# A woven four-layer transformer kernel: one shared round order replaced by an order of its own per engine, with the back half first

## The chip, the cores and the metric

The kernel runs on one core of one Trainium2 chip. The metric is the device time of one launch in microseconds. Before the change it is 4669.69 us, the median of 3 runs (4665.78 to 4671.7). A difference is given against that median.

## What is computed

Input are 16 sequences of 256 tokens with 128 features, and the weights of eight residual steps, taken one after another:

```python
x = L0_attn_x
x = x + _L0_attn_ref(_layernorm(x), ...)   # causal softmax attention, 16 heads of 8
x = x + _L0_ffn_ref(_layernorm(x), ...)    # top-2 of 8 experts with a capacity, hidden 512
x = x + _L1_attn_ref(_layernorm(x), ...)   # causal softmax attention
x = x + _L1_ffn_ref(_layernorm(x), ...)    # shared-key attention (4 heads) and top-2 of 8 gated experts
x = x + _L2_attn_ref(_layernorm(x), ...)   # causal linear attention (relu)
x = x + _L2_ffn_ref(_layernorm(x), ...)    # causal softmax attention and a gated MLP
x = x + _L3_attn_ref(_layernorm(x), ...)   # attention with weights (1 + arccos(cos))**-3.2
x = x + _L3_ffn_ref(_layernorm(x), ...)    # three blocks: linear + LoRA, layernorm, gelu, linear + LoRA
```

All matrices are float32. A sequence needs nothing of another one.

## The kernel before

Two sequences (512 tokens) make a pass, and there are 8 passes. Features lie on the 128 partitions, tokens along the free side. The work of a pass is cut in two **halves**, each with buffers of its own and four of the eight PSUM banks (the class Half): the **front** half holds the first four residual steps (stages causal0, moe0, causal1, mqa and moe1, list FRONT, L182), the **back** half the last four (linear, causal2, mlp, arccos, qlora and block0 to block2, list BACK, L184). Front hands its sum to back at its end (L1432 writes back_x). `run` (L1524) writes, for each engine, front of pass 0 alone, then a loop of 7 turns that holds front of pass i+1 and back of pass i, then back of pass 7 alone. In a turn the two halves depend on each other only at the end of the turn, where front writes back_x for the next turn.

The halves meet on the same three engines. TensorE (PE) runs all matmuls, ScalarE (ACT) exponentials, copies and table functions, VectorE (DVE) maxima, masks and sums. Every engine executes its instructions in the order in which they were written, so the order in which the two halves' instructions are written decides who waits for whom. Each half is a set of generators, one for each stage and engine (`headed_pe`, `arccos_act` and so on), that yield a **round number** before each group of instructions. SHARES (L169) gives a weight to each kind of round, PHASES (L170) says how many rounds a stage has. `schedule` (L189) lays the rounds of both halves on one axis from 0 to 1 by these weights and sorts them; `weave` (L204) lets each half write all its instructions up to that round. The sorted list is the same for all three engines. So both halves advance in proportion and end together.

The stages that matter here: a causal stage first takes the row maxima of all scores (`max_pe` L583 on PE, reductions L627 on DVE), then 12 weights sets (`causal_scores_pe` L657: scores, an exponential on ACT at L767, then `causal_pv_pe` L685). moe0 has 16 rounds (`moe0_pe` L1326) of two matmuls into the hidden layer (L1338), two relus on ACT (L1359) and two matmuls out (L1346). arccos works on four **units** (half the heads of one sequence): `arccos_act` (L1099) runs six passes over a buffer of 4096 columns for each unit, a logarithm (L1134), tanh, square root and arctangent (L1132), a logarithm and an exponential, each of which needs the one before. Functions of different tables need a table load between them. When the six passes of a unit are done, DVE sums the buffer (`arccos_sums_dve` L1137) and PE multiplies with the values (`arccos_pv_pe` L1085, L1094). The two buffers alternate between the units.

At the start SyncE issues all loads (`load`, L1540) in the order masks, const, input of pass 0, causal0, lora, the integer weights, then the other stages, qlora last. PE first multiplies the LoRA factors (L1593), and DVE builds the effective weights weff from the integer weights, the scales and that product (L1624 to L1632). PE waits for weff and for the qlora load before it starts on front of pass 0, though only the back half reads them:

```python
            last.then_inc(lora_ps, 1)
            pe.wait_ge(weff_ready, 1)
            pe.wait_ge(loaded["qlora"], 16)
            run(pe, {...
```

Of the kernel before, what the change touches and what calls it, by code (L numbers as in the profile page):

```python
# [107 lines left out]
class Signal:  # L108
# [56 lines left out]
NORM_ROUNDS = 2  # L165
PROJECT = 3
ROUTE = 5
OUT = 3
SHARES = {"norm": 1, "project": 3.14, "maxima": 2.36, "weights": 0.98, "linear": 2, "out": 1.38, "queries": 1.5, "route": 1.8, "experts0": 1.8, "experts1": 1.2, "mlp": 1.2, "arc_in": 2.3, "arc": 2.3, "block": 1}  # L169
PHASES = {  # L170
    "norm": [(NORM_ROUNDS, "norm")],
    "causal": [(PROJECT, "project"), (MROUNDS + 1, "maxima"), (CSETS + 1, "weights"), (OUT, "out")],
    "linear": [(PROJECT, "project"), (ESETS + 1, "linear"), (OUT, "out")],
    "mqa": [(1, "project"), (TILES + 1, "maxima"), (QSETS, "queries"), (3, "out")],
    "moe0": [(ROUTE, "route"), (FSETS + 1, "experts0")],
    "moe1": [(ROUTE, "route"), (EXPERTS + 2, "experts1")],
    "mlp": [(5, "mlp")],
    "arccos": [(6, "arc_in"), (UNITS * ARC_STEPS + 2, "arc"), (OUT, "out")],
    "block": [(3 + NORM_ROUNDS, "block")],
}  # L180
ROUNDS = {kind: sum(n for n, _ in phases) for kind, phases in PHASES.items()}
# [7 lines left out]
def schedule(halves):  # L189


    order = []
    for h, parts in enumerate(halves):
        times = [SHARES[phase] for kind, _ in parts for n, phase in PHASES[kind] for _ in range(n)]
        at = 0.0
        for r, time in enumerate(times):
            order.append(((at + time / 2) / sum(times), h, r))
            at += time
        if parts is FRONT:
            order[-1] = (1.0, h, r)  # L200
    return [(h, r) for _, h, r in sorted(order)]
# [10 lines left out]
def in_rounds(parts, turn, stage_of):  # L212

    first = 0
    for kind, name in parts:
        for r in stage_of[kind](turn, name):
            yield first + r
        first += ROUNDS[kind]

# [164 lines left out]
def build(nc, x_dram, w_dram, qw_dram, out_dram):  # L384
    cols, width = columns()
    with ExitStack() as ctx:
# [50 lines left out]
        def norm_pe(pe, h, turn, n, first=0):  # L437
# [7 lines left out]
            if gain:  # L445
                pe.wait_ge(loaded[gain], 16)
# [1298 lines left out]
```

## Time and profile before

| | |
|---|---|
| median of 3 runs | 4669.69 us (4665.78 to 4671.7) |
| profiled execution, its own time | 4677.62 us |
| its span, first to last instruction | 4675.8 us |
| busy in the span: PE, ACT, DVE | 3620.7, 2342.1, 1741.4 us |
| front of pass 0 alone, first matmul to the loop | 34.87 to 403.70 us |
| 7 turns of the loop | 403.70 to 4294.37 us |
| back of pass 7 alone | 4294.37 us to the end |
| mean granted TensorE clock | 0.787 of full |

The table is read from the page of the profile and from the timeline of PE: the loop starts and ends where the first matmul of the back half (L442 on back_x) starts. DMA matters only in the first 35 us; after that 1 to 6 GB/s are moved.

### The profile page before, as it was taken

The page shows a single profiled execution, that of the slowest core. Times are in us where ns is not written, and L with a number is a line of the kernel's source. Part 1 is how long each engine was busy: PE and PEld are TensorE (multiplying, and loading weights), DVE is VectorE, ACT ScalarE, POOL GpSimd, SP SyncE. Part 2 cuts the span into 40 slices and gives each one's busy share as a digit, 9 for nine tenths or more (in the row PEclk, how much of TensorE's full clock was granted, in tenths as well). Part 3 has the DMA queues.
Part 4 walks back from the last instruction along what each step waited for, and adds up shares of the span by engine and source line. Part 5 has one row for each costly group of instructions (what it writes and reads, how often), then busy time and mean ns, then how long its engine had stood idle before and what let it go on. Part 6 is the DMA issues. An engine that isn't in the chain of part 4 may idle for free.

```text
span 4675.8 us, 48868 instructions
## 1 busy us (share of the span) xinstructions
PE 3620.7 (77%) x19372; PEld 1949.4 (42%) x19372; DVE 1741.4 (37%) x2541; ACT 2342.1 (50%) x2177; POOL 3.8 (0%) x11
## 2 busy tenths in 40 slices
PE   5878886788767987678977888678876798767834
PEld 2445443454334543335434444345433454333411
DVE  2225333343433434344243533334343343433332
ACT  2223348543684436743475435844368443674275
POOL 0000000000000000000000000000000000000000
PEclk8858896788867897588966989578886779858766
DMA  2000000000000000000000000000000000000000
GB/s 113 1 1 3 1 1 1 0 6 1 1 1 5 1 1 1 1 6 1 1 1 1 6 1 1 1 0 6 1 1 1 3 1 1 1 1 3 1 0 3
DMA packets 4578, 20.31 MB, mean 4 GB/s; under 512 B 608, under 2 KB 864, under 8 KB 3808
## 3 DMA queue, kind: packets, MB, share of 16 engines
q1 hardware_dynamic: 4320, 16.79, 0.9%
q8 instruction: 171, 2.80, 0.3%
q14 instruction: 87, 0.71, 0.1%
HBM read 14.70 MB, written 2.10 MB: 4 GB/s over the span
## 4 chain that ended last, share of the span: by engine, by line
PE 57%; ACT 22%; DVE 12%; issue 8%; DMA 1%; SPq 0%; DVEq 0%; ACTq 0%
ACT back_cosines L1132 6%; PE front_ps L1338 5%; PE front_ps L1346 5%; PE front_ps L1226 3%; PE back_ps L1094 3%; ACT back_cosines L1134 3%; PE front_ps L1388 3%; PE back_ps L724 2%; DVE back_nsum L1141 2%; ACT L1132 2%; PE back_ps L821 2%; PE front_ps L975 2%; ACT L1521 2%; PE front_ps L693 2%; PE back_ps L516 2%
## 5 line engine op out<-in xcount | busy, mean ns | idle before, releaser
L1132 ACT ACTIVATE back_cosines<-back_cosines 128x4096 f32<-128x4096 f32 x128 | 462.7, 3615 | 1.4
L767 ACT ACTIVATE front_scratch<-front_ps 128x1152 f32<-128x1152 f32 (+1 forms) x192 | 196.1, 1021 | 207.9 <-PE front_ps L679 207.7
L1359 ACT ACTIVATE front_scratch<-front_ps,wts 128x512 f32<-128x512 f32 x256 | 173.4, 686 | 192.4 <-PE front_ps L1338 190.4
L1134 ACT ACTIVATE back_cosines<-back_cosines,wts 128x4096 f32<-128x4096 f32 x64 | 236.9, 3701 | 63.0 <-DVE back_cosines L1189 62.8
L1338 PE MATMUL front_ps<-front_xn,wts 128*128 128x512 f32 x512 | 247.3, 606 | 9.3 <-DVE front_qk L1322 8.5
L627 DVE TENSOR_REDUCE front_negm<-front_ps 128x4 f32<-128x1024 f32 (+1 forms) x192 | 228.4, 1219 | 61.5 <-PE front_ps L601 60.3
L1346 PE MATMUL front_ps<-front_scratch,wts 128*128 128x512 f32 x512 | 240.5, 592 | 0.0
L668 PE MATMUL front_ps<-ident_bf,mask_q 128*128 128x256 bf16 x512 | 114.3, 338 | 129.8 <-ACT front_scratch L767 88.5
L532 ACT ACTIVATE back_cosines<-back_ps,wts 128x512 fp32r<-128x512 f32 (+1 forms) x136 | 120.6, 887 | 174.1 <-PE back_ps L516 41.9
L733 PE MATMUL back_ps<-zero_bf,ident_bf 128*128 128x512 bf16 x128 | 63.3, 495 | 176.7 <-DVE back_vs L1150 160.3
L532 ACT ACTIVATE front_scratch<-front_ps,wts 128x512 fp32r<-128x512 f32 (+1 forms) x152 | 128.6, 860 | 135.1 <-PE front_ps L608 60.7
L1141 DVE TENSOR_REDUCE back_nsum<-back_cosines 128x8 f32<-128x2048 f32 x64 | 143.2, 2281 | 114.0 <-ACT back_cosines L1132 114.0
L1226 PE MATMUL front_ps<-wts,front_wtok 128*128 128x128 f32 x1024 | 165.3, 338 | 23.4 <-ACT front_qk L1248 17.7
L1226 PEld LDWEIGHTS front_ps<-wts,front_wtok 128*128 128x128 f32 x1024 | 165.2, 254 | 38.5 <-ACT front_qk L1248 19.4
L1189 DVE TENSOR_SCALAR back_cosines<-back_ps 128x2048 f32<-128x2048 f32 x64 | 146.4, 2287 | 90.8 <-PE back_ps L1075 90.8
L767 ACT ACTIVATE back_cosines<-back_ps 128x1152 f32<-128x1152 f32 (+1 forms) x96 | 98.3, 1024 | 157.3 <-PE back_ps L679 157.3
L1094 PE MATMUL back_ps<-back_cosines,back_vs 128*9 128x256 f32 x1024 | 168.8, 489 | 0.0
L1371 DVE SCALAR_TENSOR_TENSOR front_scratch<-front_ps,wts,front_qk 128x512 f32<-128x512 f32 x64 | 48.0, 750 | 318.1 <-PE front_ps L1346 318.1
L1388 PE MATMUL front_ps<-front_xn,wts 128*128 128x512 f32 x288 | 151.0, 651 | 18.4 <-DVE front_qk L1322 13.0
L693 PE MATMUL front_ps<-front_scratch,front_v 128*18 128x256 f32 x1024 | 160.2, 507 | 4.4 <-ACT front_scratch L767 4.1
L595 PE MATMUL front_ps<-front_qkr 32*128 32x256 f32 (+1 forms) x1024 | 136.2, 371 | 30.0 <-DVE front_negm L627 26.5
L781 ACT ACTIVATE back_cosines<-back_ps 128x512 f32<-128x512 f32 x64 | 38.2, 597 | 220.3 <-PE back_ps L724 220.3
(310 smaller groups left out, 6857.4 us busy)
## 6 DMA issues: line engine op xcount, KB each, us to landing
wts<-w_dram SPq DMA_DIRECT2D x1, 4124.0 KB, 19.1
front_xin<-x_dram SPq DMA_DIRECT2D x8, 256.0 KB, 2.7
out_dram<-back_z SPq DMA_DIRECT2D x8, 256.0 KB, 2.0
wts<-w_dram SPq DMA_DIRECT2D x3, 640.0 KB, 20.2
wts<-w_dram SPq DMA_DIRECT2D x1, 1736.5 KB, 23.9
back_cosines<-w_dram SPq DMA_DIRECT2D x1, 1152.0 KB, 9.6
wts<-w_dram SPq DMA_DIRECT2D x1, 1101.5 KB, 5.1
wts<-w_dram SPq DMA_DIRECT2D x1, 640.5 KB, 26.1
```

The lines of the kernel that those rows point to most:

```text
L532: nc.scalar.activation(high.bitcast(F32R), ps, ACT.Copy, scale=C(sign)).then_inc(done.sem, 1)
L627: nc.vector.tensor_reduce(into, h.ps[:, js, :].rearrange("p j (g k) -> p j g k", k=keys), AX.X, ALU.max, negate=True).then_inc(h.max_done. ...
L693: nc.tensor.matmul(h.ps[rows(j, V2), 3, b * SEQ:(b + 1) * SEQ], h.v18[:, 2 * b, GROUPS * j + g, :], h.probs[:, e % 2, k * HEADW:k * HEADW ...
L767: nc.scalar.activation(h.probs[:, e % 2, 0:n * HEADW].rearrange("p (k c) -> p k c", c=HEADW), h.ps[:, 0:n, 0:HEADW], ACT.Exp, scale=float( ...
L1094: last = nc.tensor.matmul(h.ps[rows(2 * (u % 2) + g2, V1), 2 + j // 2, j % 2 * SEQ:(j % 2 + 1) * SEQ], h.vs[:, kt, HPG * g2 + j, :], h.cos ...
L1132: nc.scalar.activation(cosines, cosines, func, scale=scale).then_inc(h.arc_pass.sem, 1)
L1134: nc.scalar.activation(cosines, cosines, func, scale=scale, bias=C(bias)).then_inc(h.arc_pass.sem, 1)
L1141: nc.vector.tensor_reduce(h.nsum[:, kt, :].rearrange("p (g2 j) -> p j g2", g2=2), h.cosines[:, u % 2, kt * 4 * TOK:(kt + 1) * 4 * TOK].rea ...
L1226: last = nc.tensor.matmul(h.ps[:, e % BANKS if n > 1 else 3, t * P:(t + 1) * P], h.wtok[:, t, e:e + 1].broadcast_to([P, P]), C("ident"), s ...
L1338: nc.tensor.matmul(h.ps[:, c, :], w1[:, k * P:(k + 1) * P], h.xn[:], start=True, stop=True)\
L1346: last = nc.tensor.matmul(h.ps[:, 2 + e % 2, :], w2[:, k * P:(k + 1) * P], h.hid[:, part, c, :], start=(part + c == 0), stop=(part + c == 2))
L1388: last = nc.tensor.matmul(h.ps[:, i, :], W(s, w)[:, e * P:(e + 1) * P], h.xn[:], start=True, stop=True)
```

## The change

SHARES, PHASES, ROUNDS, `schedule` and the round numbers go. The generators now yield with no number, and at many more places: before nearly every wait of an engine. `weave` gets a table of run lengths, one for each engine, and lets front and back advance in turns by that many yields; what is left of a half when the table ends is written behind it. The tables were made so that at every wait the back half goes first if it is ready. Which instruction the three engines have next need no longer be of the same half.

Second, the loads are issued in the order in which they are used: const, masks, input, causal0, moe0, causal1, mqa, moe1, the input of pass 1, lora, the integer weights, qlora, linear, causal2, mlp, arccos. The LoRA product on PE and the making of weff on DVE move from the start to between front of pass 0 and the loop (`lora_pe`, `dequant_dve`, called by `run` as `before_back`).

No instruction of the computation is added or taken out. The core of the diff (two of the many places with a yield are shown; the others are alike):

```diff
-SHARES = {"norm": 1, "project": 3.14, "maxima": 2.36, ...}
-PHASES = {
...
+PE_RUNS = (
+    1, 2, 1, 1, 1, 2, 2, 2, 2, 1, 2, 2, 2, 10, 1, 8, 1, 8, 1, 3, 3, 1, 2, 2, 2, 3, 2, 2, 1, 1, 1, 1, 1, 2, 2, 2,
...
+ACT_RUNS = (
...
+DVE_RUNS = (
...
-def weave(order, halves):
-
-    ahead = [next(half, None) for half in halves]
-    for h, r in order:
-        while ahead[h] is not None and ahead[h] <= r:
-            ahead[h] = next(halves[h], None)
+def weave(runs, halves):
+
+    for half in halves:
+        next(half)
+    for i, steps in enumerate(runs):
+        for _ in range(steps):
+            next(halves[i % 2], None)
+    for half in halves:
+        for _ in half:
+            pass
...
                 for n, (func, scale, bias, in_table) in enumerate(steps):
-                    yield steps_first(u) + n
+                    yield
                     table(in_table)
                     if n == 0:
+                        yield
                         act.wait_ge(h.cos_ready.sem, h.cos_ready.at(turn, s, 2 * u + 2))
...
             table(None)
-            weave(schedule([FRONT]), [half(front, FRONT, Turn(None, 0))])
+            weave((), [half(front, FRONT, Turn(None, 0))])
             table(None)
+            if before_back:
+                before_back(eng)
             with eng.Fori(0, PASSES - 1) as i:
-                weave(schedule([FRONT, BACK]), [half(front, FRONT, Turn(i, 1)), half(back, BACK, Turn(i, 0))])
+                weave(runs, [half(front, FRONT, Turn(i, 1)), half(back, BACK, Turn(i, 0))])
...
+            load("const")
             load("masks")
-            load("const")
             sp.dma_start(front.xin[:], x_dram[:, 0:TOK]).then_inc(xin_loaded, 16)
-            load("causal0")
+            for s in ("causal0", "moe0", "causal1", "mqa", "moe1"):
+                load(s)
+            load_x(0, slice(TOK, 2 * TOK))
             load("lora")
             sp.dma_start(qint, qw_dram).then_inc(qint_loaded, 16)
-            for s in list(STAGES)[4:]:
+            for s in ("qlora", "linear", "causal2", "mlp", "arccos"):
                 load(s)
-            load_x(0, slice(TOK, 2 * TOK))
```

What the tables do is seen in the order of the instructions. Line numbers of the changed kernel differ; REGISTER_ALU rows are waits and counters. L1146 and L1144 are the arccos passes (before L1134 and L1132), L1386 the relu of moe0, L1362 and L1371 its matmuls, L1080 the cosines (before L1075), L1100 their product with the values (before L1094), L1528 the second linear of a block (before L1487).

**ACT in the loop, at the arccos passes.** Before, from the fifth pass of the first unit on (L532 and L767 belong to front's causal1):

```order
L1134 ACTIVATE back_cosines<-back_cosines,wts 128x4096
L532 ACTIVATE front_scratch<-front_ps,wts 128x512
L1132 ACTIVATE back_cosines<-back_cosines 128x4096
L764 REGISTER_ALU
L767 ACTIVATE front_scratch<-front_ps 128x1152
L764 REGISTER_ALU
L767 ACTIVATE front_scratch<-front_ps 128x1152
L1134 ACTIVATE back_cosines<-back_cosines,wts 128x4096
L764 REGISTER_ALU
L767 ACTIVATE front_scratch<-front_ps 128x768
L764 REGISTER_ALU
L767 ACTIVATE front_scratch<-front_ps 128x1152
```

After, at the start of the first unit:

```order
L1386 ACTIVATE front_scratch<-front_ps,wts 128x512
L1146 ACTIVATE back_cosines<-back_cosines,wts 128x4096
L1144 ACT_TABLE_LOAD
L1144 ACTIVATE back_cosines<-back_cosines 128x4096
L1144 ACT_TABLE_LOAD
L1144 ACTIVATE back_cosines<-back_cosines 128x4096
L1144 ACT_TABLE_LOAD
L1144 ACTIVATE back_cosines<-back_cosines 128x4096
L1564 ACT_TABLE_LOAD
L1146 ACTIVATE back_cosines<-back_cosines,wts 128x4096
L1144 ACTIVATE back_cosines<-back_cosines 128x4096
L1146 ACTIVATE back_cosines<-back_cosines,wts 128x4096
```

Before, 31 of front's activations stand between the 24 passes of the loop. After, none does: all 24 stand in a row, with 16 table loads between them (before 20), and 24 relus of moe0 (12 of its 16 rounds) stand ahead of them, 8 behind. In the whole loop 34 table loads became 33.

**PE in the loop, at the same place.** After, from the fourth of the eight groups of cosines to the product of the third unit with the values:

```order
L1358 REGISTER_ALU
L1362 MATMUL front_ps<-front_xn,wts 128x512 x2
L1371 MATMUL front_ps<-front_scratch,wts 128x512 x2
L1080 MATMUL back_ps<-back_qkr 128x256 x8
L1093 REGISTER_ALU
L735 MATMUL back_ps<-zero_bf,ident_bf 128x512
L1100 MATMUL back_ps<-back_cosines,back_vs 9x256 x8
L735 MATMUL back_ps<-zero_bf,ident_bf 128x512
L1100 MATMUL back_ps<-back_cosines,back_vs 9x256 x8
L1080 MATMUL back_ps<-back_qkr 128x256 x16
L735 MATMUL back_ps<-zero_bf,ident_bf 128x512
L1100 MATMUL back_ps<-back_cosines,back_vs 9x256 x8
```

Then follow, without a row of front, the second half of that product, the cosines and the product of the third unit. Before, 277 of front's 955 matmuls of a turn stand between the fourth group of cosines and the third unit's product (its maxima, weights, and the projections of mqa); after, none does.

**PE at the end of the loop.** After, the last matmul of the back half and what follows it:

```order
L693 MATMUL front_ps<-front_scratch,front_v 18x256 x3
L696 MATMUL front_ps<-front_scratch,front_v 18x128 x3
L1528 MATMUL back_ps<-back_sq,weff 128x512
L664 REGISTER_ALU
L667 MATMUL front_ps<-ident_bf,mask_q 128x2x128 x3
L673 MATMUL front_ps<-front_qkr 128x256 x3
L678 MATMUL front_ps<-front_maxTr,max_rows 128x256 x3
L673 MATMUL front_ps<-front_qkr 128x128 x3
L678 MATMUL front_ps<-front_maxTr,max_rows 128x128 x3
```

345 of front's 955 matmuls (from the fourth weights set of causal1 to the end of moe1) stand behind back's last one. Before, a single one did, as the end of the loop's order on PE shows:

```order
L1388 MATMUL front_ps<-front_xn,wts 128x512 x2
L1392 REGISTER_ALU
L1393 MATMUL front_ps<-front_scratch,wts 128x512
L1487 MATMUL back_ps<-back_sq,weff 128x512
L1385 REGISTER_ALU
L1392 REGISTER_ALU
L1393 MATMUL front_ps<-front_scratch,wts 128x512
```

## Rows read from the trace of the kernel before

**Rows 1.** Timeline of PE, back's first matmul in turns 1, 3, 4 and alone.

```profile
403.70 1.22 PE L442 MATMUL back_ps<-back_x,wts 128*128 128x512 f32 x1 [2.45 <-DVE back_x L1432]
1511.51 1.22 PE L442 MATMUL back_ps<-back_x,wts 128*128 128x512 f32 x1 [5.27 <-issue]
2071.46 1.22 PE L442 MATMUL back_ps<-back_x,wts 128*128 128x512 f32 x1 [5.45 <-issue]
4294.37 1.22 PE L442 MATMUL back_ps<-back_x,wts 128*128 128x512 f32 x1 [2.86 <-DVE back_x L1432]
```

**Rows 2.** Windows, third turn: length, PE, PEld, DVE, ACT, POOL busy, clock, DMA, GB/s.

```profile
1511.51:1773.22 261.71, 235.75 (x1419) 134.28 (x1419) 92.48 (x139) 101.24 (x130) 0.00 (x0) 0.87 0.01 2
1773.22:1803.00 29.78, 23.84 (x68) 10.67 (x68) 15.95 (x17) 19.60 (x24) 0.00 (x0) 1.00 0.00 1
1803.00:1990.50 187.50, 129.03 (x766) 69.16 (x766) 73.51 (x90) 138.57 (x78) 0.00 (x0) 0.61 0.00 1
1990.50:2071.46 80.96, 59.75 (x172) 29.37 (x172) 34.52 (x72) 34.00 (x42) 0.00 (x0) 0.88 0.01 4
```

**Rows 3.** The same view, front alone (four rows), then back alone (four).

```profile
34.87:189.25 154.38, 124.86 (x606) 64.71 (x607) 40.07 (x66) 48.57 (x60) 0.00 (x0) 0.85 0.00 1
189.25:251.57 62.32, 50.75 (x213) 23.51 (x212) 25.58 (x28) 15.24 (x18) 0.00 (x0) 0.74 0.00 0
251.57:403.70 152.13, 115.38 (x538) 68.29 (x535) 40.94 (x87) 34.53 (x45) 0.00 (x0) 0.69 0.00 0
34.87:202.46 167.59, 136.50 (x632) 69.55 (x633) 44.06 (x71) 52.69 (x66) 0.00 (x0) 0.86 0.00 1
4294.37:4492.93 198.56, 146.97 (x838) 79.77 (x838) 65.57 (x80) 66.05 (x82) 0.00 (x0) 0.75 0.00 1
4492.93:4601.25 108.32, 23.43 (x150) 7.94 (x150) 33.35 (x33) 107.72 (x40) 0.00 (x0) 0.59 0.00 0
4601.25:4671.84 70.59, 42.25 (x80) 11.79 (x80) 14.53 (x20) 17.73 (x22) 0.00 (x0) 0.62 0.00 0
4294.37:4460.70 166.33, 128.04 (x787) 71.59 (x787) 51.70 (x68) 53.17 (x66) 0.00 (x0) 0.74 0.00 1
```

**Rows 4.** Timeline of ACT, back alone: first unit of arccos: start, length in us.

```profile
4492.93 3.71 ACT L1134 ACTIVATE back_cosines<-back_cosines,wts 128x4096 f32<-128x4096 f32 x1 [7.54 <-DVE back_cosines L1189]
4496.66 1.28 ACT L1132 ACT_TABLE_LOAD   x1
4497.95 3.62 ACT L1132 ACTIVATE back_cosines<-back_cosines 128x4096 f32<-128x4096 f32 x1
...
4520.00 3.69 ACT L1134 ACTIVATE back_cosines<-back_cosines,wts 128x4096 f32<-128x4096 f32 x1
```

**Rows 5.** Timeline of ACT in the third turn, between two passes.

```profile
1841.90 3.70 ACT L1134 ACTIVATE back_cosines<-back_cosines,wts 128x4096 f32<-128x4096 f32 x1
1845.50 0.80 ACT L767 ACTIVATE front_scratch<-front_ps 128x768 f32<-128x768 f32 x1
1850.71 3.62 ACT L1132 ACTIVATE back_cosines<-back_cosines 128x4096 f32<-128x4096 f32 x1
```

**Rows 6.** Busy time by windows, in the middle of the third turn.

```profile
1680.00:1760.00 80.00, 74.73 (x427) 36.88 (x426) 17.28 (x37) 36.14 (x49) 0.00 (x0) 1.00 0.00 1
```

**Rows 7.** Timeline of DVE and PE at the start.

```profile
8.30 0.48 DVE L1621 MEMSET back_x<- 128x512 f32 x1
13.19 0.56 DVE L1624 CAST weff<-back_cosines 128x768 f32<-128x768 int32 x1 [4.41 <-DMA back_cosines<-qw_dram]
15.38 0.95 DVE L1632 TENSOR_TENSOR weff<-weff,back_ps 128x768 f32<-128x768 f32 x1
34.87 2.05 PE L442 MATMUL front_ps<-front_x,wts 128*128 128x512 f32 x2 [19.64 <-DMA wts<-w_dram]
```

**Rows 8.** Timeline of DVE at the end of the second turn.

```profile
1508.36 0.69 DVE L1432 TENSOR_TENSOR back_x<-front_x,front_z 128x512 f32<-128x512 f32 x1
1511.59 0.43 DVE L480 COPY front_x<-front_xin 128x512 f32<-128x512 f32 x1 [2.54 <-issue]
```

More of the change, by code:

```diff
@@ L162 @@
 FSETS = EXPERTS * 2
[L165 to L169, printed above, removed]
-PHASES = {
[L171 to L181, printed above, removed]
+PE_RUNS = (
[4 rows of a table added]
+)
+ACT_RUNS = (
[3 rows of a table added]
+)
+DVE_RUNS = (
[3 rows of a table added]
+)
 FRONT = [("norm", "causal0"), ("causal", "causal0"), ("norm", "moe0"), ("moe0", "moe0"), ("norm", "causal1"),
@@ L186, with in_turn @@
         ("block", "block0"), ("block", "block1"), ("block", "block2")]
[L189 to L201, printed above, removed]
-def weave(order, halves):
-    ahead = [next(half, None) for half in halves]
-    for h, r in order:
-        while ahead[h] is not None and ahead[h] <= r:
-            ahead[h] = next(halves[h], None)
-def in_rounds(parts, turn, stage_of):
-    first = 0
+def weave(runs, halves):
[7 more added lines that the diff above has]
+            pass
+def in_turn(parts, turn, stage_of):
     for kind, name in parts:
-        for r in stage_of[kind](turn, name):
-            yield first + r
-        first += ROUNDS[kind]
+        yield from stage_of[kind](turn, name)
 class Half:
@@ L728, in linear_scores_pe @@
                 if e > 0:
-                    linear_pv_pe(pe, h, turn, s, e - 1)
+                    yield from linear_pv_pe(pe, h, turn, s, e - 1)
         def clear_ps(bank):
@@ L867, in headed_act @@
             if s in CAUSAL:
-                yield from max_act(act, h, turn, s, PROJECT + MROUNDS)
+                yield from max_act(act, h, turn, s)
                 yield from causal_exp_act(act, h, turn, s)
@@ L900, in mqa_norm_dve, with mqa_out_pe @@
                 .then_inc(h.y_ready.sem, 1)
[L903 to L904 removed]
+        def mqa_out_pe(pe, h, turn, s):
+            yield
             pe.wait_ge(h.y_ready.sem, h.y_ready.at(turn, s, PAIR))
@@ L1598, in _ @@
             pe.wait_ge(loaded["qlora"], 16)
-            run(pe, {"norm": norm_pe, "causal": headed_pe, "linear": headed_pe, "mqa": mqa_pe, "moe0": moe0_pe,
-                     "moe1": moe1_pe, "mlp": mlp_pe, "arccos": arccos_pe, "block": block_pe})
+        @block.tensor
+        def _(pe):
+            pe.wait_ge(loaded["const"], 16)
+            pe.wait_ge(consts_ready, CONSTS)
+            run(pe, PE_RUNS, {"norm": norm_pe, "causal": headed_pe, "linear": headed_pe, "mqa": mqa_pe, "moe0": moe0_pe,
+                     "moe1": moe1_pe, "mlp": mlp_pe, "arccos": arccos_pe, "block": block_pe}, lora_pe)
         @block.scalar
```

384 lines of the change are left out of this document (222 added, 162 removed), and 9 rows, old and new, of tables (ACT_RUNS, DVE_RUNS, PE_RUNS).

## The prediction

> **What bounds the kernel now.** I first read the timeline of PE for the first back matmul of each turn, since a turn is what repeats. The loop runs from 403.70 to 4294.37 us [rows 1], so a turn takes 3890.7 / 7 = 555.8 us. Outside it lie front of pass 0 (34.87 to 403.70) and back of pass 7 (from 4294.37), each alone. The kernel therefore holds both halves undisturbed, and next I read the busy time by windows there and in the third turn. Alone, front needs 368.8 us from its first matmul to the hand-over and back 377.5 us to its last additions [rows 1, 3]. In the loop both together take 555.8. What the weave is worth is the difference, 190 us a turn.
>
> Two kinds of stretch make up the turn [rows 2]. In the first 261.7 us (linear, causal2 and mlp against causal0 and moe0) PE is busy for 235.8 us, 90%: it bounds. From 1803.0 to 1990.5 back runs the arccos passes; PE is busy 129.0 of 187.5 us and ACT 138.6 of 187.5. The passes are a chain on ACT: alone, a unit is six passes of 3.6 to 3.7 us and table loads of 1.28 us, with nothing between [rows 4], and the four units with their sums take 108.3 us in which PE is busy for 23.4 [rows 3]. In the loop front's exponentials stand between the passes [rows 5]; the passes take longer, but front gets through causal1 and mqa beside them. This is the reader's main point: PE's cheapest free time is under the passes.
>
> **The change part by part.** The computation is the same on every engine, so only the order costs or gains.
>
> *The passes.* The changed order puts all 24 passes of a turn on ACT in a row. Front stands in moe0, where each round needs two relus of ACT, and 8 of them are queued behind the passes; PE gets no front matmul between the fourth group of cosines and the third unit's product. So front stands still for the passes, and PE idles for most of them. What front did there before must be done elsewhere. At the end of the turn 345 front matmuls stand behind back's last one: front runs alone from the fourth weights set of causal1 to the end of moe1. A turn thus has four stretches, and each has its row:
>
> A, turn start to the first pass. Back moves through 4294.37 to 4492.93 of its lone run (198.6 us, PE busy 147.0), front through 34.87 to 189.25, to within a round of the thirteenth of moe0 (154.4 us, PE busy 124.9) [rows 3]. PE has 271.8 us to do. For the rate I take the like stretch of the old turn: 261.7 us for what keeps PE busy 136.5 + 128.0 = 264.5 us alone [rows 2, 3], a factor of 0.989. A = 0.989 x 271.8 = 269 us.
>
> P, the passes and back's products between them: 108 us, as alone [rows 3].
>
> C, last pass to back's last matmul. Back alone 70.6 us, PE busy 42.3; front from 189.25 to 251.57 (62.3 us, PE busy 50.8) [rows 3]. By the same factor 92 us. Both lone rows were at a lower clock (0.62 and 0.74) than a woven stretch of this kind, which had 0.88 [rows 2], so the work shrinks; back's chain of 70.6 is the floor. I take 88, nearer to the first, since PE has 93 us to do.
>
> D, front alone: 251.57 to 403.70, 152 us, PE busy 115.4 at clock 0.69 [rows 3].
>
> Sum: 269 + 108 + 88 + 152 = 617 us, against 555.8: 61 us more in each turn, 7 x 61.5 = 430 us in all. The order with back in front lets back's chain run at nearly its lone pace, but a turn ends with front, and this tail is what is late next.
>
> *More yields.* They place single instructions differently and cost none. The gain they could bring is that PE in A is busier than 90%; it is a bound, below. The loop has one table load fewer (33 for 34, 1.28 us [rows 4]): 9 us at most over the run, hidden or not, taken as nothing.
>
> *Table loads.* Alone, the pass behind a load starts 1.29 us after the load did and the load right after the pass before [rows 4]. The Trainium skill (ScalarE: Activation LUTs, What ACT_TABLE_LOAD costs) gives about 1283 ns for the load and another 1380 ns of drain with every switch of set. By that rule the 16 loads of a row of passes would cost 22 us more, P would be 130 and the run 155 us longer, an estimate from that page. The trace has the 1.28 and not the drain; P stays.
>
> *Loads and the start.* PE now waits until 34.87 for the last loads [rows 7]. After, it needs const, the input and front_x. DVE's preparations end at 8.78 [rows 7], the copy to front_x is another 0.43 [rows 8], so the first matmul starts near 9.7: 25.1 us earlier. The input load is third and causal0 fourth in the queue, and causal0 is needed 8 us later; were they late, the gain falls, at worst to nothing. In return weff is made between front and the loop: 13.19 to 16.33 on DVE [rows 7], 3.1 us, which nothing hides, since DVE comes to it only after writing back_x, and PE waits. Entering a turn costs 2.5 us from back_x to the next instruction when nothing hides it [rows 8]; up to that is added. I take 4.5. PE's six LoRA products fit beside DVE's steps. Net -20.6 us; bounds -22 and +6.
>
> **Result.** Profiled execution 4677.6 + 430 - 20.6 = 5087 us. It was 7.9 above the median of the runs, so 5080 us as a median, 8.8% slower.
>
> **Bounds.** A below: the old stretch was at clock 0.87 [rows 2], that is, 26% of the time at the lower of the two levels (1.2 and 2.4 GHz); with PE at the high level throughout, as in 80 us of its middle (clock 1.00, PE busy 74.7 of 80) [rows 6], it shrinks by up to 13%, to 234. A above: by lone times instead of busy times, 0.784 x (198.6 + 154.4) = 277, and 290 if the fixed orders make engines wait for each other. P: 108 to 112. C: 71 to 100. D: 116 (all at the high level, 31% off the busy 115.4) to 155. For 8 in 10 I let A be 258 to 277, C 80 to 95, D 145 to 152: turns of 591 to 633, that is 4900 to 5190 us.
>
> **The rivals.**
>
> 1. *PE is granted more.* The denser A and C run at the high level, D partly. For it speaks that the middle of the old turn had 1.00; against it that the early part, equally dense in matmuls, did not, as the mean of 0.87 shows, and that D follows a lone pattern that had 0.69. A 240, C 75, D 145 make 568 and 4677.6 + 85 - 20.6 - 7.9 = 4734 us. Between this and 4900 I put 0.14. The Trainium skill (Perfetto Trace Analysis, Matmul Optimizations) says that the matmul engine scales with its use, so matmuls belong back to back in batches. By that rule A gains and P and D lose; the rows at 0.59 and 0.69 agree for the last two.
>
> 2. *The other side: back's priority pays.* Back's chain bounds A and C at 198.6 + 70.6 = 269, and front's work fits in PE's gaps. It decides at the point where A + C falls under 555.8 + 3 - 108 - 152 = 299 us, while PE has 365 us of lone busy time to do there; it must be done in 82% of its lone time with no gap. With everything at its low bound a turn takes 234 + 108 + 71 + 116 = 529, the run 4677.6 - 188 - 20.6 - 7.9 = 4461 us. A mild form (A + C = 290) gives 4590. Chance 0.05.
>
> 3. *The orders jam.* Each engine's order is fixed and made from durations that the chip need not keep; a front instruction ahead of a ready back one then holds both. A 285, C 98, D 152 make 643 and 5260 us. Chance above 5190: 0.09.
>
> 4. *Both cancel.* A + C comes out within 1.3 us of 299, and the run stays at 4670. Nothing in the rows picks that point. Chance 0.02.
>
> **How the numbers follow.** Forecast (4900 to 5190) 0.70, rival 1 0.14, rival 2 0.05, rival 3 0.09, rival 4 0.02. The range 4900 to 5190 leaves out 3 in 10, so I take its ends to 4820 and 5240, which takes in half of rivals 1 and 3 each: 0.70 + 0.07 + 0.04 = 0.81. Within 0.2% of the old time, 9 us, is about what a measurement of this kernel can tell from no change: 0.02. Faster: 0.05. Slower: 0.93.
>
> **What would show it.** Right: the 24 passes of a turn back to back within about 108 us, PE busy for about a quarter of them; a tail of 150 us after back's last matmul with back silent; turns of about 617 us; the first front matmul near 10 us. Each step is wrong if: A is outside 258 to 277 us; front matmuls run on PE during the passes; the tail is under 140 us; ACT waits inside a row of passes. The whole is wrong if A + C is under 299 us.

## The result, and the profile after

The changed kernel takes 4813.06 us (4803.85 to 4827.78, 4 runs), the one before 4667.73 us beside it; the ratio is 1.0317 with a 95% interval of 1.0283 to 1.035. It is slower, as predicted, but by 3.2% and not by 8.8%: the time lies 267 us under the 5080 forecast and 7 us below the range of 4820 to 5240.

The timeline of PE shows where turns start, as in [rows 1]; the first row is the start of the kernel, the last is the lone back half.

```profile
9.23 1.19 PE L429 MATMUL front_ps<-front_x,wts 128*128 128x512 f32 x1 [9.23 <-DVE front_x L474]
379.51 1.22 PE L429 MATMUL back_ps<-back_x,wts 128*128 128x512 f32 x1 [4.18 <-DVE weff L1667]
956.81 2.08 PE L429 MATMUL back_ps<-back_x,wts 128*128 128x512 f32 x2 [5.85 <-DVE front_x L474]
1537.66 2.08 PE L429 MATMUL back_ps<-back_x,wts 128*128 128x512 f32 x2 [6.46 <-issue]
2114.81 2.07 PE L429 MATMUL back_ps<-back_x,wts 128*128 128x512 f32 x2 [6.48 <-issue]
4414.49 2.07 PE L429 MATMUL back_ps<-back_x,wts 128*128 128x512 f32 x2 [2.42 <-DVE back_x L1468]
```

Seven turns take 4414.49 - 379.51 = 4034.98 us, 576.4 us each, where 617 were predicted and 555.8 stood before [rows 1]. The loop starts 24.2 us earlier.

The next view is that of [rows 2]: busy time by windows, third turn of the changed kernel, cut at the first pass, the end of the last pass and back's last matmul. These are the prediction's stretches A, P, C and D. The columns are length, then busy us and instructions of PE, PEld, DVE, ACT and POOL, clock, DMA share, GB/s.

```profile
1537.66:1762.47 224.81, 210.71 (x1433) 122.03 (x1434) 101.80 (x145) 107.80 (x139) 0.00 (x0) 0.95 0.01 2
1762.47:1870.70 108.23, 26.93 (x161) 9.07 (x159) 35.17 (x36) 107.64 (x41) 0.00 (x0) 0.64 0.00 0
1870.70:1958.44 87.74, 78.31 (x293) 34.35 (x293) 38.41 (x46) 35.30 (x44) 0.00 (x0) 0.80 0.00 1
1958.44:2114.81 156.37, 109.90 (x537) 66.50 (x536) 42.52 (x90) 41.78 (x52) 0.00 (x0) 0.71 0.01 3
```

Three of the four came as predicted: P 108 (108), C 88 (88), D 156 (152). A is 225 us where 269 was predicted. (PE's counts here are higher than those of the instruction order, since the trace has two records for many f32 matmuls: the 535 that start in D are the order's 345.) The old turn's stretch that served as its measure had 26.0 us of PE's idle time in 261.7 at clock 0.87 [rows 2]; A has 14.1 in 224.8 at 0.95.

The standstill of front shows on PE during the passes, in the timeline of that engine: from the last front matmul on, cosines and the product with the values, nothing of front, and an idle time of 27 us.

```profile
1767.43 0.51 PE L1080 MATMUL back_ps<-back_qkr 32*128 32x256 f32 x8
1794.90 0.61 PE L735 MATMUL back_ps<-zero_bf,ident_bf 128*128 128x512 bf16 x1 [26.96 <-DVE back_vs L1165]
1795.44 3.59 PE L1100 MATMUL back_ps<-back_cosines,back_vs 128*9 128x256 f32 x16
```

On the page the same stands in one row of the costliest groups, for all eight passes of the kernel:

```profile
L735 PE MATMUL back_ps<-zero_bf,ident_bf 128*128 128x512 bf16 x128 | 61.2, 478 | 492.3 <-DVE back_vs L1165 489.2
```

### The profile page after: what moved, and what is told of

Read it like the earlier page. It is cut to its first block, busy times and chain, and to the rows that moved or that the text cites. A ratio compares the mean times of both kernels' runs of the same rounds, so it can differ in the third digit from the quotient of the medians.

```text
span 4802.0 us, 48861 instructions
## 1 busy us (share of the span) xinstructions
PE 3487.6 (73%) x19372; PEld 1882.9 (39%) x19372; DVE 1752.1 (36%) x2541; ACT 2336.1 (49%) x2170; POOL 3.8 (0%) x11
## 4 chain that ended last, share of the span: by engine, by line
PE 60%; ACT 24%; DVE 10%; issue 6%; DMA 0%; DVEq 0%; ACTq 0%; SPq 0%
ACT back_cosines L1144 8%; ACT back_cosines L1146 5%; PE front_ps L1362 5%; PE front_ps L1371 4%; PE front_ps L1245 3%; PE front_ps L1418 3%; PE front_ps L987 2%; ACT L1144 2%; PE back_ps L726 2%; PE front_ps L597 2%; PE back_ps L827 2%; PE front_ps L693 2%; PE back_ps L429 2%; PE front_ps L603 2%; PE back_ps L512 1%
## 5 line engine op out<-in xcount | busy, mean ns | idle before, releaser
L1144 ACT ACTIVATE back_cosines<-back_cosines 128x4096 f32<-128x4096 f32 x128 | 462.9, 3617 | 2.1
L735 PE MATMUL back_ps<-zero_bf,ident_bf 128*128 128x512 bf16 x128 | 61.2, 478 | 492.3 <-DVE back_vs L1165 489.2
L1362 PE MATMUL front_ps<-front_xn,wts 128*128 128x512 f32 x512 | 263.3, 640 | 135.9 <-ACT front_scratch L1386 122.4
L1386 ACT ACTIVATE front_scratch<-front_ps,wts 128x512 f32<-128x512 f32 x256 | 171.5, 684 | 222.4 <-PE front_ps L1362 220.4
L1371 PE MATMUL front_ps<-front_scratch,wts 128*128 128x512 f32 x512 | 246.5, 605 | 0.0
L1146 ACT ACTIVATE back_cosines<-back_cosines,wts 128x4096 f32<-128x4096 f32 x64 | 236.9, 3702 | 8.2 <-DVE back_cosines L1207 7.5
L735 PEld LDWEIGHTS back_ps<-zero_bf,ident_bf 128*128 128x128 bf16 x128 | 12.8, 100 | 528.6 <-DVE back_vs L1165 495.4
L1362 PEld LDWEIGHTS front_ps<-front_xn,wts 128*128 128x128 f32 x512 | 98.1, 200 | 258.0 <-ACT front_scratch L1386 134.2
L1245 PEld LDWEIGHTS front_ps<-wts,front_wtok 128*128 128x128 f32 x1024 | 154.8, 242 | 81.5 <-DVE front_wtok L1342 43.7
L1436 ACT ACTIVATE front_scratch<-front_ps 128x512 f32<-128x512 f32 x72 | 43.0, 597 | 249.5 <-PE front_ps L1418 249.5
L1100 PE MATMUL back_ps<-back_cosines,back_vs 128*9 128x256 f32 x1024 | 162.4, 474 | 0.0
L597 PE MATMUL front_ps<-front_qkr 32*128 32x256 f32 (+1 forms) x1024 | 141.0, 370 | 26.9 <-ACT front_v L553 13.7
L1371 PEld LDWEIGHTS front_ps<-front_scratch,wts 128*128 128x128 f32 x512 | 101.0, 197 | 129.4 <-issue 129.4
L533 DVE SCALAR_TENSOR_TENSOR front_split_parts<-front_ps,wts,front_scratch 128x512 fp32r<-128x512 f32 x64 | 48.0, 750 | 273.9 <-ACT front_scratch L529 273.9
```

Source lines behind the costliest of these rows:

```text
L597: nc.tensor.matmul(h.ps[:, j, gi * keys:(gi + 1) * keys], h.q4r[rows(j, QUAD), g0 + gi, b * SEQ + qt * P:b * SEQ + (qt + 1) * P], h.k4r[ro ...
L1100: last = nc.tensor.matmul(h.ps[rows(2 * (u % 2) + g2, V1), 2 + j // 2, j % 2 * SEQ:(j % 2 + 1) * SEQ], h.vs[:, kt, HPG * g2 + j, :], h.cos ...
L1144: nc.scalar.activation(cosines, cosines, func, scale=scale).then_inc(h.arc_pass.sem, 1)
L1146: nc.scalar.activation(cosines, cosines, func, scale=scale, bias=C(bias)).then_inc(h.arc_pass.sem, 1)
L1245: last = nc.tensor.matmul(h.ps[:, e % BANKS if n > 1 else 3, t * P:(t + 1) * P], h.wtok[:, t, e:e + 1].broadcast_to([P, P]), C("ident"), s ...
L1362: nc.tensor.matmul(h.ps[:, c, :], w1[:, k * P:(k + 1) * P], h.xn[:], start=True, stop=True)\
```

## Experiments

All ratios are to the kernel before, run beside it. A turn is the mean of the seven. "Idle" is a window's length less PE's busy time. The traces of experiments 1 to 7 and 9 lack most records of the bf16 matmuls that clear a bank with zeros (L735; 12 in a stretch A, 2.8 us of PE's busy time in the changed kernel's third turn). Where busy and idle times of two kernels are set against each other below, "without the zero matmuls" says that they are left out of both; lengths and clocks are not touched by it.

### 1. The new start alone

```diff
@@ kernel before, SyncE @@
-            load("masks")
             load("const")
+            load("masks")
             sp.dma_start(front.xin[:], x_dram[:, 0:TOK]).then_inc(xin_loaded, 16)
-            load("causal0")
+            for s in ("causal0", "moe0", "causal1", "mqa", "moe1"):
+                load(s)
...
@@ run @@
+            if before_back:
+                before_back(eng)
             with eng.Fori(0, PASSES - 1) as i:
```

> The kernel before with the new start alone: weights loaded in order of use, LoRA products and dequantization between the lone front and the loop; the weave is that of before. Both theories of the weave expect the loop to start 24 us earlier, as in the changed kernel (379.5 us for 403.7), turns of 555.8 us as before, and about 4644 us in all (ratio 0.995). If the gain were given back (a late transfer, or weff behind which back waits), the ratio would be 1.000 with a longer first turn.

4652.74 us, ratio 0.9956 (0.9932 to 0.9979); 0.44% of 4675 is 20.6 us, and the interval goes from 10 to 32. The timeline of PE at the start and at the first turn:

```profile
9.32 1.19 PE L442 MATMUL front_ps<-front_x,wts 128*128 128x512 f32 x1 [9.32 <-DVE front_x L480]
383.73 1.22 PE L442 MATMUL back_ps<-back_x,wts 128*128 128x512 f32 x1 [4.14 <-DVE weff L1624]
```

The first matmul comes 25.6 us earlier [rows 7], and the loop 20.0 us earlier: 5.6 us are given back between them, where weff now stands and back waits for it. The prediction had 25.1 and 4.5. The loop starts 4 us later than expected: the changed kernel has the same wait for weff (4.18 us) and gives back 1.5 us only, as front alone takes 370.3 us there for 374.4 here. The start is a small gain of its own; the slowdown is in the loop (7 x 20.6 = 144 us) and, with 6 us, in the lone back half (387.6 us for 381.5), whose order did not change. A turn of this profile takes 558.3 us, with the weave of the kernel before and its 555.8: so far can two profiles of one weave lie apart, and differences of 2 or 3 us a turn say nothing.

### 2. Back first, but in the old rounds

The rounds of the kernel before in one list for all engines, sorted as the changed kernel's PE comes to them.

```diff
@@ kernel before @@
+ROUND_RUNS = (
+    0, 1, 1, 1, 1, 1, 1, 1, 1, 1, 1, 1, 1, 4, 1, 4, 2, 2, 1, 1, 1, 2, 1, 1, 2, 2, 1, 1, 1, 1, 1, 1, 1, 1, 1, 1, 1,
...
 def schedule(halves):
...
+    for i, rounds in enumerate(ROUND_RUNS):
+        for _ in range(rounds):
+            order.append((i % 2, at[i % 2]))
+            at[i % 2] += 1
```

> The kernel before with its rounds in one list for all engines, but listed in the order in which the changed kernel's PE comes to them (back first). So PE's sequence of halves is the changed one as far as rounds allow, without the yields at every wait and without an order of its own for each engine. Theory 1 (the fine yields and the own orders are what made stretch A, turn start to first arccos pass, cheap): A is 255 to 275 us at a clock near 0.87, the turn about 600 to 617 and the run 5.5% or more slower than before. Rival (the sequence of halves on PE made A cheap): A is 220 to 235 us at a clock near 0.95, and the turn is about 577 us, 3 to 4% slower than before.

5019.92 us, ratio 1.0757 (1.0715 to 1.08), a turn of 603.4 us. Its third turn by windows, A to D:

```profile
1614.48:1874.58 260.10, 232.30 (x1422) 134.04 (x1434) 102.89 (x145) 106.62 (x136) 0.00 (x0) 0.85 0.01 2
1874.58:1987.38 112.80, 36.29 (x172) 13.86 (x174) 36.15 (x37) 112.21 (x48) 0.00 (x0) 0.67 0.00 0
1987.38:2072.38 85.00, 68.39 (x275) 29.32 (x277) 37.15 (x44) 30.13 (x37) 0.00 (x0) 0.82 0.00 0
2072.38:2218.54 146.16, 102.36 (x533) 61.47 (x536) 42.79 (x90) 34.01 (x46) 0.00 (x0) 0.78 0.01 3
```

The same matmuls stand in A (1434 weight loads in both) and take 35 us more. Without the zero matmuls that is 10.9 us of idle time (27.8 for 16.9) and 24.4 us of busy time (232.3 for 207.9) at a clock of 0.85 for 0.95. So theory 1 holds against its rival: the sequence of the halves did not make A cheap, the fine yields and own orders did. What the prediction had costed was this kernel, near enough: a turn of 603 us for the 617.

### 3. Front ahead of a pass on ACT

The tables of the changed kernel, with one rule added: a ready front step of ACT goes ahead of a pass. Of the tables this is the start of ACT's:

```diff
@@ changed kernel @@
 ACT_RUNS = (
-    1, 3, 2, 3, 3, 5, 3, 4, 2, 1, 1, 22, 2, 3, 2, 1, 2, 2, 14, 2, 2, 2, 2, 2, 1, 2, 2, 5, 2, 5, 2, 2, 3, 5, 2,
+    0, 1, 1, 2, 2, 3, 3, 5, 3, 4, 1, 1, 1, 1, 1, 24, 2, 2, 1, 1, 12, 2, 3, 2, 2, 2, 1, 2, 1, 3, 1, 2, 2, 2, 2,
...
```

> The changed kernel with other tables: back first when ready as there, except on ACT, where a ready front step goes ahead of an arccos pass. Stretch A should stay at 225 us. If the standstill of front behind 24 contiguous passes is what makes the changed kernel slow, the passes take about 125 us for 108, the lone front tail shrinks from 156 to about 115 us, and a turn is about 535 us: some 4.5 to 6.5% faster than the changed kernel and 2.5 to 3.5% faster than before. Rival (work put under the passes costs PE as much as it saves, since PE runs there at the lower clock): the turn stays above 560 us, at least as slow as before.

4449.40 us, ratio 0.9521 (0.9486 to 0.9556), a turn of 525.7 us. Windows of its third turn, A to D, and ACT's timeline between two passes:

```profile
1434.95:1647.25 212.30, 195.04 (x1391) 115.02 (x1402) 98.72 (x141) 102.42 (x130) 0.00 (x0) 0.95 0.01 2
1647.25:1772.27 125.02, 83.35 (x338) 34.11 (x339) 60.05 (x65) 123.26 (x65) 0.00 (x0) 0.79 0.00 1
1772.27:1845.12 72.85, 58.76 (x382) 27.07 (x386) 19.45 (x28) 39.05 (x49) 0.00 (x0) 0.87 0.00 1
1845.12:1960.64 115.52, 82.81 (x294) 52.25 (x294) 38.07 (x84) 18.78 (x26) 0.00 (x0) 0.69 0.01 3
```

```profile
1653.42 3.62 ACT L1146 ACTIVATE back_cosines<-back_cosines 128x4096 f32<-128x4096 f32 x1
1656.95 1.25 ACT L1388 ACTIVATE front_scratch<-front_ps,wts 128x512 f32<-128x512 f32 x2
1658.21 1.28 ACT L1146 ACT_TABLE_LOAD   x1
```

Front's activations between the passes, mostly two relus of 1.25 us together, cost P 16.8 us; PE does 83 us of work in it for 27, and A, C and D lose 12.5, 14.9 and 40.9. The gain is larger than expected (7.6% under the changed kernel by the medians, for 4.5 to 6.5). The tables were made anew over the whole turn, so they also moved front's point at the first pass: A is 212 and not the 225 expected, with 1402 weight loads for 1434, and how much of the gain is that of the one rule alone is not shown. The rival (work under the passes costs PE what it saves) falls.

### 4. Both halves ending together

At every wait the half that is further behind goes first, by the same kind of tables.

```diff
@@ changed kernel @@
 ACT_RUNS = (
-    1, 3, 2, 3, 3, 5, 3, 4, 2, 1, 1, 22, 2, 3, 2, 1, 2, 2, 14, 2, 2, 2, 2, 2, 1, 2, 2, 5, 2, 5, 2, 2, 3, 5, 2,
+    1, 3, 2, 3, 3, 4, 1, 1, 2, 2, 2, 2, 1, 9, 2, 4, 2, 2, 2, 3, 4, 2, 3, 3, 2, 3, 3, 1, 2, 1, 2, 1, 17, 2, 1, 6,
...
```

> The changed kernel with other tables: at every wait the half that is further behind goes first, so that both halves end the turn together; front goes ahead of a pass on ACT. The new start, the yields and the computation are those of the changed kernel. If fine yields save PE's short waits everywhere and the lone tail was the whole loss, a turn is 510 to 525 us and the run about 4360 to 4450 us (ratio to before 0.935 to 0.955). Rival (the high level of PE's clock is a share that is granted whatever the packing, about 0.81 in the loop in both kernels): PE's 431 us of busy time and its idle time bound the turn at about 540 to 550, ratio 0.97 to 0.99.

4373.56 us, ratio 0.9365 (0.9331 to 0.9399), a turn of 514.8 us. No tail is left (8.7 us, A 288.8 at clock 0.93, P 124.6, C 90.3 in the third turn). The rival (PE's busy time and its waits bound the turn at 540 us, at a granted clock that stays about 0.81) falls too: the loop was granted 0.84, and PE is busy for 406 us of the third turn, for 439 before, both without the zero matmuls.

### 5. The old priority with the new yields

Tables by the share of its lone time that each half has done, which is the rule of the order before.

```diff
@@ changed kernel @@
 ACT_RUNS = (
-    1, 3, 2, 3, 3, 5, 3, 4, 2, 1, 1, 22, 2, 3, 2, 1, 2, 2, 14, 2, 2, 2, 2, 2, 1, 2, 2, 5, 2, 5, 2, 2, 3, 5, 2,
+    1, 3, 2, 3, 3, 4, 1, 1, 2, 2, 2, 2, 1, 8, 2, 1, 2, 2, 4, 2, 3, 2, 2, 3, 5, 2, 2, 2, 2, 4, 3, 1, 2, 1, 2, 1,
...
```

> The changed kernel with other tables: at every wait the half that has done the smaller share of its lone time goes first, which is the order of the kernel before (both halves spread evenly over the turn), but with the yields at every wait and an order of its own for each engine. It completes a square: before (even, coarse) 556 us a turn, coarse back first 604, changed (back first, fine) 577. Theory 1 (the fine yields and own orders save 25 to 35 us a turn under any priority; back first costs the rest): the turn is 520 to 530 us, the run 4400 to 4480 us, ratio 0.945 to 0.96. Rival (the fine yields pay only where back first crowds stretch A): the turn is 545 to 556 us and the ratio 0.98 to 1.0.

4407.24 us, ratio 0.9433 (0.9403 to 0.9463), a turn of 518.2 us. With it the square is complete (us a turn), but for one thing: the order before is not quite met. In the third turn 44.9 us of front stand behind back's last matmul, where before it was 6.3, and 19 of front's activations between the passes for 31.

| | rounds, one list | yields at every wait, own lists |
|---|---|---|
| halves in proportion | 555.8 (before) | 518.2 |
| back first | 603.4 | 576.4 (changed) |

The finer weave saves 37.6 us under the old priority, a little more than the 25 to 35 expected and in part perhaps by that other order, and 27.0 under the new one. Putting back first costs 47.6 in rounds and 58.2 in the fine weave. The change did both at once and shows the difference, +20.6.

### 6. Fine on PE only

The tables of the changed kernel for PE; ACT and DVE keep to the rounds of experiment 2.

```diff
@@ changed kernel @@
 ACT_RUNS = (
-    1, 3, 2, 3, 3, 5, 3, 4, 2, 1, 1, 22, 2, 3, 2, 1, 2, 2, 14, 2, 2, 2, 2, 2, 1, 2, 2, 5, 2, 5, 2, 2, 3, 5, 2,
+    0, 2, 2, 3, 3, 5, 3, 5, 3, 1, 1, 21, 1, 3, 4, 4, 14, 1, 2, 2, 2, 4, 3, 5, 2, 4, 2, 3, 3, 4, 2, 3, 3, 2, 2,
...
 DVE_RUNS = (
-    1, 1, 1, 2, 2, 3, 3, 2, 3, 1, 4, 4, 2, 3, 2, 4, 4, 1, 4, 1, 4, 3, 4, 3, 2, 12, 2, 18, 2, 2, 2, 4, 4, 2, 3,
+    2, 2, 1, 3, 3, 3, 3, 1, 4, 6, 4, 6, 8, 1, 4, 1, 5, 4, 1, 14, 2, 12, 2, 6, 2, 2, 2, 2, 2, 2, 3, 2, 3, 1, 1,
...
```

> The changed kernel with PE's table as it is, while ACT and DVE follow the one list of rounds of the coarse back-first run. It tells whose order saves in stretch A (260 us coarse, 225 changed). If PE's own sequence is what saves, A is 225 to 232 us. If ACT and DVE hold PE up when they keep to rounds, A is 245 to 260 us. In both cases the passes, which front's ACT steps now interrupt a little, take about 113 us, and the lone tail about 150.

4855.92 us, ratio 1.0377 (1.0331 to 1.0422), a turn of 583.7 us. Stretch A in the third and the fifth turn:

```profile
1564.06:1801.39 237.33, 213.25 (x1423) 124.14 (x1434) 102.58 (x145) 106.36 (x137) 0.00 (x0) 0.93 0.01 2
2711.03:2959.07 248.04, 224.74 (x1423) 129.43 (x1434) 102.67 (x145) 106.47 (x137) 0.00 (x0) 0.88 0.01 2
```

Its idle time is 24 us, between the coarse 27.8 and the changed kernel's 16.9 (without the zero matmuls), so most of the waits that the finer weave saves go only if ACT and DVE leave the rounds too. The time does not follow the waits: PE's own order alone saves 19.7 of the 27.0 us a turn (583.7 for 603.4, the changed kernel 576.4), 14 of them in A and 7 in C in the mean of the seven turns. A is 237 to 250 us, in four turns within the second expectation and in three between the two, and the turns of one order differ by 12 us: the clock is between 0.93 and 0.87. Whether PE's gain comes from the more numerous yields or from a list of its own was not taken apart.

### 7. PE kept busy under the passes

```diff
@@ changed kernel, arccos_pv_pe @@
+            if u < UNITS - 1:
+                busy_pe(pe, h, turn, s, u, 36 if u else 60)
             pe.wait_ge(h.vs_ready.sem, h.vs_ready.at(turn, s, u + 1))
...
+            for _ in range(count):
+                nc.tensor.matmul(h.ps[:, 2, :], ident_bf[:], zero_bf[:].broadcast_to([P, TOK]), start=True, stop=True,
+                                 skip_group_check=True)
```

> The changed kernel with idle work for PE beside the arccos passes: 60, 36, 36 and 36 bf16 matmuls of zeros into an empty bank, in the four gaps in which PE waits for ACT (27, 16, 16 and 16 us). Nothing waits for them, and they should end before the passes do. If the granted clock follows how busy PE was just before (the reading that made A cheap: PE at 0.94 there), the clock under the passes rises from about 0.65 to over 0.8, and stretch C behind them, 88 us with PE busy 78 at about 0.80, becomes 75 to 82 us; a turn is 5 to 12 us shorter (ratio to the changed kernel about 0.985). Rival (the clock does not answer to such work, or the extra work only delays): C stays at 86 us or more and the turn at 577 or above.

4808.67 us, ratio 1.0287 (1.0254 to 1.032), which can't be told from the changed kernel's 1.0317; a turn of 579.3 us. P and C of its first turn, then P and C of the changed kernel's:

```profile
609.56:717.89 108.33, 67.73 (x323) 26.43 (x327) 35.16 (x36) 107.73 (x41) 0.00 (x0) 0.83 0.00 1
717.89:805.89 88.00, 79.33 (x291) 34.89 (x293) 38.50 (x46) 35.22 (x43) 0.00 (x0) 0.79 0.00 0
```

```profile
605.25:713.57 108.32, 27.01 (x161) 9.09 (x159) 35.16 (x36) 107.73 (x41) 0.00 (x0) 0.64 0.00 0
713.57:801.56 87.99, 79.72 (x293) 34.96 (x293) 38.51 (x46) 35.20 (x43) 0.00 (x0) 0.79 0.00 1
```

The clock under the passes rose from 0.64 to 0.83, and in this turn C did not move. In the other six turns C was 80 us for 88, as expected, but then A was 232 to 240 instead of 225, and the turn was not shorter. The changed kernel has the same pair in two of its own turns with no idle work (the second: A 236.9, C 79.7). So raising the clock under the passes bought no time, and what it did to C is not shown: the expectation of a shorter turn fell, and the rival's turn of 577 or more held.

### 8 and 9. Waits put back, short and long

The coarse weave has more waits and a lower clock in A. To see whether one brings the other, waits go back into the changed kernel with the order untouched. Short ones: PE waits for its own last matmul, 48 times in A. Long ones: PE waits for DVE or ACT after every fourth round, 12 times.

```diff
@@ short: max_pe, and the same in causal_pv_pe @@
                 last.then_inc(h.max_ps.sem, 1)
+                if s != "causal1":
+                    pe.wait_ge(h.max_ps.sem, h.max_ps.at(turn, s, m + 1))
@@ long: max_pe, and with probs_ready in causal_scores_pe @@
                 last.then_inc(h.max_ps.sem, 1)
+                if s != "causal1" and m % 4 == 3:
+                    pe.wait_ge(h.max_done.sem, h.max_done.at(turn, s, m + 1))
```

> The changed kernel with short waits of PE put back: after each round of causal0's and causal2's maxima and after each of their value products PE waits for its own last matmul (48 waits in stretch A, none in the passes or behind them; the order stays). By the distance between a matmul's end and what its signal releases, some 0.3 to 0.4 us each, they should bring about the 14 us of idle time that the coarse run has more than the changed kernel in A. Theory 1a (the granted clock answers to PE's short waits): besides the idle time PE's busy time in A rises by 10 us or more from 211, the clock in A falls from 0.94 to 0.90 or less, and A is 248 to 262 us. Rival (idle time costs only itself; the clock in A is set by something else in the order): busy stays at 211 and the clock at 0.93 or more, and A is 232 to 243 us.

> The changed kernel with twelve longer waits of PE put back in stretch A: after every fourth round of causal0's and causal2's maxima PE waits until DVE has reduced it, and after every fourth set of their weights until ACT has taken the exponentials. Such waits of 0.8 to 2 us, not the short ones tried before, are what the coarse run has more of. Theory 1b (waits of this length take the clock down): idle time in A rises by 10 to 18 us from 14, busy time by 10 us or more from 211, the clock is 0.90 or less, and A is 245 to 265 us. Rival (waits cost themselves alone, and the level granted is set by something that no single wait decides): busy stays within 5 us of 211, the clock at 0.93 or more, and A is 232 to 245 us.

Short: 4874.83 us, ratio 1.0409 (1.0368 to 1.045), a turn of 586.0. Long: 5014.15 us, ratio 1.0744 (1.0708 to 1.0781), a turn of 604.0. Stretch A of the third turn, the short waits first:

```profile
1558.85:1797.28 238.43, 219.60 (x1433) 122.83 (x1434) 102.47 (x146) 108.00 (x139) 0.00 (x0) 0.93 0.01 2
```

```profile
1596.75:1853.16 256.41, 223.97 (x1422) 127.52 (x1434) 102.83 (x146) 108.03 (x139) 0.00 (x0) 0.87 0.01 2
```

The 48 short waits cost 13.6 us, 0.28 each: 4.7 us of idle time (18.8 for 14.1) and 8.9 us of busy time (219.6 for 210.7), at a clock of 0.93 for 0.95. Theory 1a fell, and the rival held by its 232 to 243 us and its clock, but not by its busy time, which was to stay at 211. By the clock, 11 us more of A are at the lower level, which is worth some 5 us of PE's work (an estimate); the rest of the 8.9 is unexplained. The idle time is a third of the 14 us expected: the 0.3 to 0.4 us put between a matmul's end and what its signal releases was too long, as most of PE's added idle times are under 0.2 us. So the experiment brought neither the idle time nor, with it, a fair test of 14 us in short pieces.

The 12 long waits brought, without the zero matmuls, 15.8 us of idle time (32.7 for 16.9) and with it 15.8 us of busy time (223.7 for 207.9) for the same matmuls, at a clock of 0.87: theory 1b held. This kernel has the changed order and the time of the coarse one, 604.0 and 603.4 us a turn. It is not shown that the length of the single wait decides: the long waits also brought three times the idle time of the short ones. Nor does either explain the coarse weave alone, which has a lower clock (0.85) with fewer idle times of 0.8 us or more in A: 14, for 19 here and 7 in the changed kernel. Two of the long waits in the timeline of PE:

```profile
1717.83 0.79 PE L597 MATMUL back_ps<-back_qkr 32*128 32x256 f32 x4 [1.39 <-DVE back_cosines L632]
1726.04 0.79 PE L597 MATMUL back_ps<-back_qkr 32*128 32x256 f32 x4 [1.30 <-ACT front_scratch L775]
```

### 10. The version that beats both

The balanced tables of experiment 4, searched further by moving single steps.

```diff
@@ changed kernel @@
 ACT_RUNS = (
-    1, 3, 2, 3, 3, 5, 3, 4, 2, 1, 1, 22, 2, 3, 2, 1, 2, 2, 14, 2, 2, 2, 2, 2, 1, 2, 2, 5, 2, 5, 2, 2, 3, 5, 2,
+    0, 1, 1, 2, 2, 3, 3, 2, 3, 2, 2, 2, 1, 11, 2, 3, 1, 3, 2, 1, 1, 2, 3, 1, 1, 2, 3, 1, 2, 2, 2, 2, 1, 1, 2, 2,
...
```

> A second balanced order, the one before it searched further by moving single steps on each engine, for the version that beats both kernels. By both theories a turn of 505 to 515 us for the 514 of the first balanced order, and a run of 4310 to 4375 us, ratio 0.925 to 0.937. If the searched order rests on durations that the chip does not keep, an engine waits in the middle and the turn is above 520.

4348.31 us, ratio 0.9287 (0.9249 to 0.9326): 6.7 to 7.5% under the kernel before, and 9.7% under the changed one by the medians. The time and the ratio are as expected, the turn is just over its 505 to 515: it takes 516.7 us in the profiled execution, which at 4379.4 us of span was above the median of its runs. Whether it beats experiment 4, whose interval it just misses, was not measured side by side.

## Why the prediction was right in its sign and wrong in its size

*Stretches P and D: right.* The 24 passes stand in a row for 108.2 us, as alone, with PE busy for 26.9 of them (alone 23.4) [rows 3]. The front tail is 156 us, 152 predicted. The old turn's passes were read too wide: they run from 1810.3 to 1974.1, 163.8 us and not 187.5 [rows 2], but no term rests on it.

By the Trainium skill's rule of a drain with each table load (ScalarE: Activation LUTs, What ACT_TABLE_LOAD costs) P would be 130, an estimate from that page. The trace of the changed kernel disagrees with its 108.2, and agrees with the page's 1283 ns for the load itself: 1.28 us.

*Stretch C: right.* 88 us predicted, 79.7 to 88.0 measured, the lower value in two turns of seven.

*The start: right.* Net -20.6 us predicted; the loop starts 20.0 us earlier when it was made alone, 24.2 in the changed kernel.

*Stretch A: the step that failed.* The prediction took "a factor of 0.989" from the old turn's stretch and made A = 0.989 x 271.8 = 269 us. Measured are 222 to 237 us, 227 in the mean of the seven turns, a factor of 0.84. By the prediction's own sign, A outside 258 to 277 us, the step is wrong. Seven times the 42 us is 292 us, a little more than the whole miss of 283: the sum stood at 5087 us for a profiled execution, which took 4803.85. The other terms nearly cancel, in the mean of the seven turns C with -2.6 us, D with +3.4 and P with +0.3 (+8 us in all), the lone back half with +6, the start with -4.

The factor was that of a weave in rounds, and for one it nearly holds: the coarse run has 259 us in the mean (0.953). The 10 us between 269 and 259 are no matter of yields; the one turn that gave the factor was itself long, 298.8 us from its start to the first pass for 294.9 in the mean of the old seven. The prediction wrote of the added yields that they "place single instructions differently and cost none", named the gain that PE is busier than 90%, and gave it no value in the sum. It is worth 32 us a turn in A (259 to 227 in the mean), 27.0 in the whole turn. In the third turn 10.9 us of the 35 are waits no longer made, and 24.4 are busy time, at a clock of 0.85 in rounds and 0.95 in the fine weave. Experiment 9 shows that twelve long waits put into the unchanged order bring 15.8 us of busy time back; that the same waits are what the coarse weave loses by is argued, not shown.

*Rival 1, "PE is granted more": right for A, wrong for the rest.* It had A 240, C 75 and D 145. A was granted 0.95 in the third turn and came out below it; C is 85 in the mean, and D kept its lone pattern at 0.71. Against it I had held that the old turn's early part was as dense and had 0.87. It was as full of matmuls, but not as free of waits (26.0 us idle in 261.7, for 14.1 in 224.8). Of the rule that matmuls belong back to back (Trainium skill, Perfetto Trace Analysis, Matmul Optimizations) the long waits are an instance, 0.87 for 0.95; the short ones, 0.93, hardly.

*The other side, "back's priority pays": wrong,* as predicted. A + C was 313 us and had to be under 299. (Its mild form was summed wrongly: A + C = 290 makes a turn of 550 and 4608 us, not 4590.) Priority for back costs 58.2 us a turn in the fine weave, and the mechanism is the one given: front stands still under the passes and is late at the end.

*What stays open.* Why the clock is 0.88 in one turn and 0.95 in the next of the same order (below), and whether the length of the waits or their sum matters. Of the busy time in A, 8.6 us lie between the coarse run and that with long waits (232.3 and 223.7, without the zero matmuls); their cause was not tried.

## What to carry to other kernels

When a change does two things at once, cost each against the kernel without the other: here the finer weave was worth -27 to -38 us a turn and the new priority +48 to +58, and only their sum was visible. A rate taken from the old kernel's stretch carries its waits and its clock with it, so it may not be used for a change that takes waits away. A long chain on one engine should let the other half's short steps in between its links, where the engine that bounds the rest would else be idle: here (experiment 3) the chain took 16.8 us more and the turn 51 us less.

## What the runs showed of the hardware

The same order can be granted two clocks. In experiment 10, turns 2 and 3, the same stretch of PE, 42 to 87 us after the turn's start:

```profile
929.76:974.76 45.00, 45.00 (x340) 32.34 (x339) 18.61 (x22) 11.30 (x16) 0.00 (x0) 0.63 0.00 1
1452.40:1497.40 45.00, 44.60 (x447) 29.30 (x443) 22.21 (x28) 21.99 (x29) 0.00 (x0) 1.00 0.01 2
```

PE is busy throughout both, mostly at 1.2 GHz in the first and at 2.4 GHz in the second, and does 340 matmuls or 447. The turns take 522.6 and 505.0 us, and the profiled execution has five of the first kind or near it and two of the second. So one turn can be 17 us longer than the next of the same order, and the six runs of this kernel lie 49 us apart (4331.9 to 4381.2), 7 us a turn. A difference in clock between two orders counts only if it holds over the turns. That of experiment 9 does: A is 255.4 to 256.5 us in all seven, at a clock of 0.87 or 0.88, where the changed kernel has 222 to 237 us at 0.89 to 0.96.

Idle matmuls on zeros raised the granted clock (0.64 to 0.83 under the passes) and bought nothing here (ratio 1.0287 for 1.0317).

A table load takes 1.28 us on ACT, and nothing more shows beside it: the pass behind it starts 1.29 us after the load did.
